# Full 128-wide slices for routed transposes, and gathers that add routed rows into x

## The reference

```
x = x + 0.5 * moe0(ln(x))      # layer 0: 16 experts, top 4, plus a shared expert
x = x + attention(ln(x))       # 16 heads of 16, causal, q k v normalised
x = x + 0.5 * moe0(ln(x))
x = x + 0.5 * moe1(ln(x))      # layer 1: 32 experts of 96, top 8, thresholded
x = x + 0.5 * ssm(ln(x))
x = x + 0.5 * moe1(ln(x))

def moe0(x):                   # E=16, K=4, I=176, SI=704
    w, idx = top_k(softmax(x @ gate_w.T), 4);  w = w / w.sum()
    combine = (one_hot(idx, 16) * w[..., None]).sum(1)
    shared = silu_mul(x @ shared_gate_up.T) @ shared_down.T * sigmoid(x @ shared_gate_vec.T)
    sparse = sum(silu_mul(x @ gate_up[e].T) @ down[e].T * combine[:, e] for e in range(16))
    return shared + sparse
```

## Time and profile before

| | us |
|---|---|
| median of 3 runs | 989.24 |
| lowest, highest | 989.04, 990.76 |
| the profiled execution's own time | 989.24 |
| span in its profile (first to last instruction) | 987.4 |
| PE busy | 888.0 |
| DVE busy | 701.0 |
| ACT busy | 493.4 |
| POOL busy | 480.5 |

### The profile page before, as it was taken

The page is one execution under the profiler, slowest core; times in us unless marked ns, Lnnn a source line. Parts: engine busy times, 40 slices in busy tenths (PEclk is TensorE's granted clock), DMA queues, the critical chain, the costliest instruction groups (busy, mean ns, idle before and its releaser), DMA issues.

```text
span 987.4 us, 20904 instructions
## 1 busy us (share of the span) xinstructions
PE 888.0 (90%) x6996; PEld 550.9 (56%) x6996; DVE 701.0 (71%) x1392; ACT 493.4 (50%) x865; POOL 480.5 (49%) x465
## 2 busy tenths in 40 slices
PE   2768889999938899899999989899999999999997
PEld 1355556666624666657665545454566445666564
DVE  6786524786789987735644898887879788875554
ACT  2856543577824577544755773344433553333322
POOL 3766267513586435277742888532433224422322
PEclk9978999999959999999999999999999999999999
DMA  9688545633121232957793542111110211112222
GB/s 304 258 220 173 122 132 124 130 77 81 61 75 64 76 72 72 223 199 138 174 191 117 159 142 85 59 52 54 43 54 23 78 50 48 54 45 87 71 69 64
DMA packets 123268, 106.63 MB, mean 108 GB/s; under 512 B 75672, under 2 KB 97944, under 8 KB 123168
## 3 DMA queue, kind: packets, MB, share of 16 engines
q1 hardware_dynamic: 117024, 88.51, 32.9%
q0 software_dynamic: 6144, 16.79, 5.9%
HBM read 58.98 MB, written 30.02 MB: 90 GB/s over the span
## 4 chain that ended last, share of the span: by engine, by line
PE 36%; DVE 5%; POOL 5%; issue 3%; ACT 1%; DMA 0%; POOLq 0%; DVEq 0%; SPq 0%; ACTq 0%
PE ps L1062 18%; PE ps L1111 9%; POOL wlo L771 2%; PE ps L1093 2%; PE ps L1037 2%; POOL hh L717 1%; POOL back L760 1%; PE ps L1255 1%; PE ps L1286 1%; PE ps L1275 1%; DVE hid L1329 1%; DVE scr L1660 1%; PE ps L1265 1%; PE ps L1079 1%; DVE hid L1337 1%
## 5 line engine op out<-in xcount | busy, mean ns | idle before, releaser
L717 POOL TENSOR_TENSOR hh<-hid,hh 128x512 f16<-128x512 f32 x120 | 144.6, 1205 | 256.0 <-ACT hh L828 255.6
L1323 DVE SCALAR_TENSOR_TENSOR hid<-gtanh,ps 128x512 f32<-128x512 f32 (+2 forms) x184 | 114.3, 621 | 153.2 <-ACT gtanh L808 150.6
L1062 PE MATMUL ps<-xhi,whi 128*128 128x512 f16 x480 | 184.5, 384 | 22.7 <-DVE hid L1323 18.5
L808 ACT ACTIVATE gtanh<-ps 128x512 f32<-128x512 f32 (+2 forms) x184 | 100.5, 546 | 193.5 <-PE ps L1062 158.3
L1062 PE MATMUL ps<-xlo,whi 128*128 128x512 f16 x480 | 184.2, 384 | 0.0
L1062 PE MATMUL ps<-xhi,wlo 128*128 128x512 f16 x480 | 184.0, 383 | 0.0
L1111 PE MATMUL ps<-whi,hh 128*128 128x256 f16 x960 | 176.3, 274 | 2.0 <-POOL hh L717 1.5
L1337 DVE SCALAR_TENSOR_TENSOR hid<-hid,ps 128x512 f32<-128x512 f32 (+2 forms) x184 | 114.4, 621 | 54.6 <-PE ps L1037 27.7
L1037 PE MATMUL ps<-whi,xs_sb 128*128 x992 | 127.9, 243 | 20.2 <-issue 13.5
L1111 PE MATMUL ps<-wlo,hh 128*128 128x256 f16 x480 | 131.4, 274 | 0.0
L828 ACT ACTIVATE hh<-hid 128x512 f16<-128x512 f32 x120 | 75.2, 627 | 110.1 <-DVE hid L1329 82.9
(11 more groups left out here) (208 smaller groups left out, 1579.5 us busy)
## 6 DMA issues: line engine op xcount, KB each, us to landing
ys_dram<-y_sb SPq DMA_DIRECT2D x60, 256.0 KB
xs_sb<-c_dram SPq DMA_DIRECT2D x64, 192.0 KB, 2.8
scr<-w_in SPq DMA_DIRECT2D x28, 384.0 KB, 4.3
scr<-we_in SPq DMA_DIRECT2D x32, 304.0 KB, 4.2
xs_sb<-c_dram SPq DMA_DIRECT2D x64, 128.0 KB, 3.0
xs_sb<-c_dram SPq DMA_DIRECT2D x64, 64.0 KB, 2.7
xs_dram<-y_sb SPq DMA_DIRECT2D x1, 3968.0 KB, 15.0
scr<-ws_in SPq DMA_DIRECT2D x8, 384.0 KB, 6.9
```

Of the source, the lines that this page charges most:

```text
L717: pool.tensor_tensor(hlo[:, k, :], hid[:, k % 2, :], hhi[:, k, :], ALU.subtract).then_inc(lo_done, 1)
L808: act.activation(gtanh[:, n % 2, 0:w], ps[:, G_BANK, 0:w], ACT.Tanh, scale=0.5 / W_SCALE)\
L1062: mm = pe.matmul(ps[:, bank, :], w[:, off:off + P], a[:, kc, t0:t0 + HN], start=(i == 0), stop=(i == 3 * KC - 1))
L1323: dve.scalar_tensor_tensor(out=hid[:, k, 0:w], in0=gtanh[:, k, 0:w], scalar=1.0, in1=ps[:, G_BANK, 0:w], op0=ALU.add, op1=ALU.mult).then_i ...
```

## The change

1. `IA` becomes 128, `IB` 48. The tile `hp` holds a block's 176 hi values, its 176 lo values and a second copy of the last 48 hi values. `turn` takes three transposes of 128 columns instead of four; the third covers lo values 96 to 175 and the hi tail. The second half of the down weights is laid out to fit, with zero rows where lo values are covered twice. All five matmuls of `down` have 128 rows.
2. ACT makes the tail copy as one more instruction a unit (semaphore `tail_done`, on which `turn` and DVE's product two units later wait).
3. The routing weight and the slot of each token travel with its row in `xs_dram`, whose rows grow from 1024 to 1056 bytes. `load_slots` on SP reads those 8 numbers back for all 31 x 128 slots, `slot_scale` on DVE picks the weight of each slot, and `y_copy` multiplies by it. As the scale differs from block to block, `y_copy` becomes an instruction per block.
4. `gather` adds its rows straight into `x` (`compute_op=ALU.add`). Four additions into one tile must follow one another, so POOL waits for the gather before on that tile. `combine`, `back` and `wk` go. The layernorm waits for the gathers themselves.
5. The routing weights are computed ahead of the send and no longer after it.
6. `ORDER` is written anew for all engines.

```diff
-IA = 112
+IA = P
@@ make_threads, route0
         put("PE", "v", "rank", q)
+        put("DVE", "r", "route_weights", q)
         put("DVE", "r", "place", q)
+        put("DVE", "r", "slot_weights", q)
         for n in range(4):
             put("POOL", "x", "send", 4 * q + n)
         put("DVE", "r", "block_experts", q)
-        put("DVE", "r", "route_weights", q)
-        put("DVE", "r", "slot_weights", q)
+        put("SP", "q", "load_slots", q)
+        put("DVE", "g", "slot_scale", q)
@@ combine
             put("POOL", "c", "gather", 8 * q + n)
-            put("DVE", "c", "combine", 8 * q + n)
@@ SP
+                elif name == "load_slots":
+                    if n:
+                        sp_.wait_ge(scale_ready, n)
+                    sp_.wait_ge(sent[n % 2], 16 * HT * K0 * (n // 2 + 1))
+                    sp_.dma_start(slot_rows[:, :, :], xs_dram.rearrange("(b p) c -> p b c", p=P)[:, :, D:D + 2 * K0])\
+                        .then_inc(slots_loaded, 16)
@@ POOL, gather
-                    if n >= 3:
-
-                        pool.wait_ge(combined, PAIR * (n - 2))
-                    for i in range(PAIR):
-                        slot, t = (PAIR * n + i) % GRING, PAIR * pair + i
-                        pool.indirect_dma_start(out=back[:, slot, :], out_offset=None, in_=ys_dram[h],
+                        pool.wait_ge(x_added[h], added(2 * (q // 2)))
+                    for t in range(PAIR * pair, PAIR * pair + PAIR):
+                        if j:
+                            pool.wait_ge(gathered[h][t], 16 * (K0 * (q // 2) + j))
+                        pool.indirect_dma_start(out=x[:, HT * h + t, :], out_offset=None, in_=ys_dram[h],
                                                 in_offset=bass.IndirectOffsetOnAxis(ap=pos[:, h, j, t:t + 1], axis=0),
-                                                bounds_check=SLOT_ROWS - 1, oob_is_err=False).then_inc(gathered[slot], 16)
+                                                bounds_check=SLOT_ROWS - 1, oob_is_err=True, compute_op=ALU.add)\
+                            .then_inc(gathered[h][t], 16)
@@ ACT, hi and y_copy
+                        act.activation(hp[:, m % 2, 0:w, 0:I0], h, ACT.Copy).then_inc(hi_done, 1)
+                        act.activation(hp[:, m % 2, 0:w, 2 * I0:2 * I0 + IB], h[:, :, IA:I0], ACT.Copy).then_inc(tail_done, 1)
@@
-                    w = xs_loads(c)
-                    act.activation(y_sb[:, m % YRING, 0:w, :], ps[:, Y_BANK + m % 2, 0:w * D].rearrange("p (b c) -> p b c", c=D),
-                                   ACT.Copy).then_inc(y_out, 1)
+                    if c == 0:
+                        act.wait_ge(scale_ready, q_of(PASSES[r][2], PASSES[r][1]) + 1)
+                    for j in range(xs_loads(c)):
+                        b = 2 * c + j
+                        ins = act.activation(y_sb[:, m % YRING, j, :], ps[:, Y_BANK + m % 2, j * D:j * D + D], ACT.Copy,
+                                             scale=sscale[:, PASSES[r][2], b:b + 1])
+                    ins.then_inc(y_out, 1)
@@ PE, turn
-                        for out, part in ((hT[:, at:at + P], hp[:, m % 2, b, 0, 0:P]),
-                                          (hT[:, at + P:at + 2 * P], hp[:, m % 2, b, 1, 0:P]),
-                                          (hT[0:IB, at + 2 * P:at + 3 * P], hp[:, m % 2, b, 0, IA:I0]),
-                                          (hT[IB:P, at + 2 * P:at + 3 * P], hp[:, m % 2, b, 1, IA:I0])):
-                            mm = pe.transpose(out, part, ident16[:, :])
+                        for i, col in enumerate((0, I0, 2 * I0 + IB - P)):
+                            mm = pe.transpose(hT[:, at + P * i:at + P * i + P], hp[:, m % 2, b, col:col + P], ident16[:, :])
@@ PE, down
-                                                                 (2, whi, P, D), (2, wlo, IB, D))):
+                                                                 (2, whi, P, D), (2, wlo, P, D))):
@@ DVE, slot_scale
+                    dve.wait_ge(slots_loaded, 16 * (n + 1))
@@ ORDER, POOL, first of its lines
-        "A4 x2 l x l x w l w2 l w2 l w2 l w2 l w2 l w l w2 l2 w l w l w l6 x l x l x l2 x l2 c2 l c l c l2 c A "
+        "A4 x2 w x l2 x l w l w4 l w l w3 l w l w2 l w l w l w l4 w l4 x l x l2 x l2 x l2 c l c l2 c l c2 l A c "
```

More of the change, by code:

```diff
@@ L39 @@
 SLOT_ROWS = NBLK * P
+ROWW = 2 * D + 4 * K0
 NRT = -(-NBLK // 2)
@@ L46 @@
 SLOTS = 12
[L47 removed]
+XRING, YRING = 3, 2
 PAIR = HT // 2
@@ L491, in build @@
         turned, hT_done, y_out = sem("turned"), sem("hT_done"), sem("y_out")
+        tail_done = sem("tail_done")
         y_stored = [sem(f"y_stored{k}") for k in range(YRING)]
-        gathered = [sem(f"gathered{k}") for k in range(GRING)]
-        combined, wk_ready, sg_ready = sem("combined"), sem("wk_ready"), sem("sg_ready")
+        gathered = [[sem(f"gathered{h}_{t}") for t in range(HT)] for h in range(HALVES)]
+        row_ready, slots_loaded, scale_ready, sg_ready = sem("row_ready"), sem("slots_loaded"), sem("scale_ready"), sem("sg_ready")
         dve_step, pool_step = sem("dve_step"), sem("pool_step")
@@ L648, in piece @@
                         rows = slice((2 * b + j) * P, (2 * b + j + 1) * P)
[L649 removed]
+                        sp_.dma_start_transpose(xs_sb[:, 2 * k + j, :, :], xs_dram16[rows, 0:2 * D])\
                             .then_inc(xs_loaded[k], 16)
+                elif name == "load_slots":
[4 more added lines that the diff above has]
+                        .then_inc(slots_loaded, 16)
                 elif name == "store_y":
@@ L1345, in piece @@
                         if s in (1, 3):
-                            dve.wait_ge(combined, PAIR * (8 * q_of(h, s - 1) + 4 * p + 4))
+                            for t in range(PAIR * p, PAIR * p + PAIR):
+                                dve.wait_ge(gathered[h][t], 16 * K0 * (1 if s == 1 else 2))
                     elif h:
@@ L1436, in piece @@
                     if n >= 2:
-                        dve.wait_ge(combined, HT * K0 * (n - 1))
+                        for t in range(HT):
+                            dve.wait_ge(gathered[h][t], 16 * K0)
                     dve.tensor_scalar(pos[:, h, :, :], ptop[:, :, 0:K0].rearrange("p t k -> p k t"), -1.0, None, ALU.add)\
@@ L1460, in piece @@
                                            ALU.mult))
-                    dve.tensor_reduce(wk[:, h, :, :], hits, AX.X, ALU.add).then_inc(wk_ready, 1)
-                elif name == "combine":
-                    q, pair, j = n // 8, n // 4 % 2, n % 4
-                    h = q % 2
-                    if n % 8 == 0:
-                        dve.wait_ge(wk_ready, q + 1)
-                        dve.wait_ge(x_added[h], added(2 * (q // 2)))
-                    for i in range(PAIR):
-                        slot, t = (PAIR * n + i) % GRING, PAIR * pair + i
-                        dve.wait_ge(gathered[slot], 16 * ((PAIR * n + i) // GRING + 1))
-                        if j:
-                            dve.wait_ge(combined, PAIR * (n - 1) + i + 1)
-                        xb = x[:, HT * h + t, :]
-                        dve.scalar_tensor_tensor(out=xb, in0=back[:, slot, :], scalar=wk[:, h, t, j:j + 1], in1=xb,
-                                                 op0=ALU.mult, op1=ALU.add).then_inc(combined, 1)
+                    if n:
+                        dve.wait_ge(sent[(n - 1) % 2], 16 * HT * K0 * ((n - 1) // 2 + 1))
+                    dve.tensor_scalar(row_pos, ptop[:, :, 0:K0], -1.0, None, ALU.add)
+                    dve.tensor_reduce(row_w, hits, AX.X, ALU.add).then_inc(row_ready, 1)
+                elif name == "slot_scale":
+                    h = n % 2
+                    dve.wait_ge(slots_loaded, 16 * (n + 1))
+                    if n >= 2:
+                        dve.wait_ge(y_out, BLOCK[RT_PASSES[n - 2]] + NRT)
+                    step(dve.tensor_tensor(slot_hit[:, :, :], slot_pos, slot_id.unsqueeze(2).to_broadcast([P, NBLK, K0]), ALU.is_equal))
+                    step(dve.tensor_tensor(slot_hit[:, :, :], slot_hit[:, :, :], slot_w, ALU.mult))
+                    dve.tensor_reduce(sscale[:, h, :], slot_hit[:, :, :], AX.X, ALU.add).then_inc(scale_ready, 1)
                 elif name == "shared_add":
@@ L1750, in lay_out @@
     dn = dn.transpose(0, 2, 1)
-    we[:, 0:IA, 2 * KC * I0:2 * KC * I0 + D] = dn[:, 0:IA]
-    for at in (0, IB):
+    we[:, :, 2 * KC * I0:2 * KC * I0 + D] = dn[:, 0:IA]
+    for at in (P - IB, P - 2 * IB):
         we[:, at:at + IB, 2 * KC * I0 + D:] = dn[:, IA:]
@@ L1773, in lay_out @@
     out["const_in"] = np.concatenate([np.eye(P, dtype=f), np.triu(np.ones((P, P), f)),
-                                      np.tile(np.arange(NBLK, dtype=f), (P, 1))], axis=1)
+                                      np.tile(np.arange(NBLK, dtype=f), (P, 1)),
+                                      np.arange(NBLK, dtype=f) * P + np.arange(P, dtype=f)[:, None]], axis=1)
     out["tau_in"], out["nu_in"] = i["L0_attn_tau"], i["L0_attn_nu"]
```

58 lines of the change are left out of this document (34 added, 24 removed), and 96 rows, old and new, of the table ORDER.

## The result

The changed kernel takes **1005.37 us** (median of 4 runs, 1002.11 to 1009.83) against 989.14 us for the kernel before in the same session (986.59 to 990.76): 1.0171 times as long, 95% interval 1.0147 to 1.0194. On another chip it was 1.0161 (1.0125 to 1.0196). Forecast were 953 us and a gain; it is a loss of 16 us. The profiled run is one of 1002.11 us with a span of 1000.3, 12.9 more than before.

What follows compares the result with a forecast made beforehand. Outside the first 66 us and the hole, TensorE's own work was taken as the bound. −36 − 5 + 3 + 3 − 1 = −36 us on a 987.4 us span gave 951.4, forecast 953; 945 to 962 at 0.45, range 932 to 984.

Steps and rivals of the forecast that it cites:

- Rival D: Down matmuls: the 0.2 us belong to a switch attention still forces, so only passes one and four gain; 965 us, chance 0.08.
- the forecast made by it, that nothing is saved: Turn's transposes on TensorE: by the skill's rule, four old ones fill only three slots, so 26.7 us less saving.
- Forecast 8, 13 without the lost cover, 10 and 10: Tile saving reaching the end in the four routed passes, of 12.9 us each; the second counts 8 after 5 lost.
- I take three quarters: Third and fourth routed passes: no single engine becomes the bound, so 10 us of 12.9 arrive in each.
- a step of the chain at 4.6 us: Adding gathers into one tile: each step costs as a plain gather, 4.6 us; eight steps a half are 37 us.
- +3 for the second half: Gathers of the second half: the last tiles come about 3 us after they could be used.
- the later end is absorbed by its earlier start: Gathers of the first half: 37 us of chain against 31 before, counted as no loss.
- Rival A: Adding gather takes twice the plain one, 9.1 us, sixteen steps on the path; 1025 us, chance 0.12 in full or part.
- its threshold, 6.9 us: Step length of an adding gather at which the slower case decides: 36 / 16 = 2.25 us more a step.
- Cover lost: Second routed pass with first attention half: seven more head pairs uncovered, 8.4 us at 61% takes 13.7; 5 us lost.
- The slot load: SP's load of slot rows, once a pass: only the first, in the first routed pass, costs; +3 us, between 0 and 11.
- The hole: TensorE's gap at 278 to 293 us: power steps now stand ahead of the last six gathers; 5 us saved, perhaps 2.

Runs made afterwards that it cites:

- the down part alone: Kernel before with one change: the down matmul on 64 rows takes 128 rows; 974.95 us, 0.9848 of the kernel before.
- the tile part: Kernel before with three full transposes, ScalarE's tail copy and five 128-row matmuls, combine steps and order as they were; 967.61 us, 0.9792 of the kernel before.
- plain gathers: Changed kernel with gathers that overwrite x, the addition left out, same waits and order; 980.96 us, 0.9914 of the kernel before.
- experiment 7: Changed kernel without slot load and scale steps; 1.0042 of the kernel before on a slower chip, 1.008 beside the changed kernel at 1.0161.
- experiment 10: Three-transpose, 128-row-matmul kernel in the old order, one power step moved ahead of two gathers, its normalise ahead of a combine; 0.9839 on a slower chip, then 0.9768.

## Why the prediction was wrong

- **Tiles: right, to the size of a block.** TensorE's timeline of the kernel after, two blocks down and one turn:

```profile
222.08 0.27 PE L1111 MATMUL ps<-whi,hh 128*128 x1
222.19 0.27 PE L1111 MATMUL ps<-wlo,hh 128*128 x1
222.30 0.38 PE L1111 MATMUL ps<-whi,hh 128*128 x2
222.52 0.27 PE L1111 MATMUL ps<-wlo,hh 128*128 x1
222.63 0.27 PE L1111 MATMUL ps<-whi,hh 128*128 x1
...
223.17 0.50 PE L1097 MATMUL ps<-ident,hp 128*128 128x128 f16 x6
```

  A block is 0.55 us, as forecast. Another turn of two blocks starts at 205.33 and the next work at 205.66: 0.33 us against 0.34 forecast. Rival D falls, whose 0.2 us would only have moved: with the down part alone, both passes that attention is woven into got shorter as well. The turn saved because two 64-column transposes among full ones cost 0.15 us on the way in and 0.18 on the way out in the trace of before, where full ones follow each other by 0.056. The pair itself starts 4 ns apart (252.558 and 252.562 us). That is what the Trainium skill says of small matmuls in separate column strips (TensorE: Matmul & The Clock Gate, "Part 3: Packing small matmuls — row/col tiling"). So the trace agrees with the rule, and the forecast made by it, that nothing is saved, failed because it left out the way in and out.
- **How much of it arrives: too much counted.** Forecast 8, 13 without the lost cover, 10 and 10. In the tile part it was 8.8 in the first routed pass, 4.6 in the second with attention, 6.4 and 3.4: 23 of the 41. The step that failed is "I take three quarters", and the 13 for the second pass. The reason given, that no engine passes 84% of a stage, isn't enough: ScalarE's tail copy cost 5 us at a busy share of 52%, and they came back when it stood in POOL's waits. What held the rest back is open. The size of the copies was right: 0.27 us for the tail and, a unit, 0.25 more for the split y copy (15.2 us over the 60 units of two blocks), where I took 0.25 for each.
- **The gathers: the step that turned the sign.** The sum took a step of the chain at 4.6 us, the value of a plain one, with +3 for the second half and nothing for the first. A step of one tile is 4.6 to 5.4 us in the rows above, but 4.6 to 6.6 over that half and 6.3 in the median of all; with plain gathers it is 5.6, as POOL's other pieces stand between. So 4.6 was too small, and mostly not because of the addition. Two more things were missing. The duration on POOL: I bounded the landing and never the 1.0 us that POOL spends on a gather; it is 1.57 now, 34 us more of POOL, worth 13. And the base: "the later end is absorbed by its earlier start" set 37 us against 31. From the first issue to the power step it was 45.7 us (154.60 to 200.35), 33.1 in the tile part, and POOL's splits of h, which TensorE's pass needs, are queued between the gathers. Rival A had the place and the sign, "POOL is blocked in order". Its price, 9.1 us a step, and its threshold, 6.9 us, were wrong: with steps 0.6 us longer than plain ones the addition cost 25 us, more than the tiles gave, and the threshold had counted on 36 us to lose and on a base of 4.6.
- **Cover lost: right mechanism, wrong size.** I took 5 us for the uncovered end of attention, seven more pairs of heads at about 1.2 us. The end went from 21 us in the tile part to 41, with TensorE 27.8 us busy at a clock of 0.69, and to 39 with plain gathers, where the pass with its attention is 14 us longer than in the tile part. So this is the price of the new order, and the addition puts 9 us on top, most of them ahead of the last gate.
- **The slot load: +3 forecast, 7 measured**, within the bounds of 0 and 11, but at another place. The first load was to cost, and "three of these run before their pass starts and are hidden". VectorE waited 1.0 us for the first, 4.3 for the second, not at all for the third and 2.6 for the fourth, and some 5 of the 7 us lie in the fourth pass.
- **The hole: right.** −5 forecast; 15.0 to 10.5 us, with both power steps ahead of the gathers.
- **A hole that I had not seen** opened at 635 us. TensorE waits 3.5 us for the routing weights of the first dense pass and then starts with its clock fallen (0.66 from 639.3 to 647 us). The stretch of 11.0 us around it is 4.6 us in the tile part and over 10 with plain gathers too, so it came with the new order.

Term by term, forecast against measured (us): tiles −41 and −21, addition and chain +3 and +25, slot load +3 and +7, order, hole and split y copy −1 (+5, −5 and −1) and +7. These measured terms give +18 where the whole change gave +16 to +17.

## What to carry to other kernels

A DMA that an engine issues costs time on that engine. Before an operation on it grows, price the issue and not only the landing, and look at what is queued behind. Work that leaves one engine for another has to be priced where it arrives: 33 us of combine steps left VectorE, 34 us came to POOL, and the kernel lost by it, though neither is its busiest engine. A new order has a price of its own, to be read in the stretch that it uncovers: here 14 us in one stage, of which the hole behind gave 6 back. A bundle of changes should be taken apart: here the half that worked on TensorE's own queue was worth 2.2%, and 2.7% once its new copy was put on the engine that was waiting anyway.

## What the runs showed of the hardware

- A gather of 128 rows of 1 KB that adds into its target holds POOL 1.57 us (median) against 1.02 and lands after 4.3 us against 3.2. The software queue has 12,288 packets for 6,144, with the 64 sends in both. In the traces a send or a plain gather has 48 packets (32 of 4 KB and 16 of 4 bytes) and a gather that adds 144 (128 of 1 KB, one a row, and 16 of 4 bytes). The Trainium skill (Perfetto Trace Analysis, "DMA Instruction — SWDGE (GPSIMD)") says that the bar of such an instruction ends when its descriptors are made and leaves out the data's movement; the trace agrees, with 1.57 us of bar and 4.3 to landing, and it shows that the addition lengthens both.
- Chips differ, and ratios move less than times. The kernel before took 988 to 989 us on some chips, at a mean granted clock of 0.969 to 0.979, and 1003 to 1004 on two others, at 0.961 to 0.973. The ratio of the tile part stayed at 0.978, but that of two other kernels, each run on a fast and a slow chip, was 0.004 (experiment 7) and 0.007 (experiment 10) higher or lower, so small differences are read between kernels on one chip.
- Two 64-column transposes into separate strips start 4 ns apart and cost 0.15 us on the way in and 0.18 on the way out among full ones that follow each other by 0.056. A 64-row matmul costs about 0.2 on either side where full ones follow each other by 0.11.
